# Experts' gathers issued two experts sooner, each in front of the additions of an earlier expert

## The reference, cut to what matters

```python
E, K, D, H, CAP = 32, 4, 512, 256, 256          # T = 8 * 1024 rows
xe = zeros((E, CAP, D)).at[e_flat, pos].set(flat[tok], mode='drop')   # up to 256 rows per expert
h  = relu2(einsum('ecd,ehd->ech', xe, up_w))    # relu, then squared
ye = einsum('ech,edh->ecd', h, down_w)
gathered = ye[e_flat, min(pos, CAP - 1)] * topk_w
routed = gathered.reshape(T, K, D).sum(axis=1)  # each row has 4 experts
out = x + gb * (routed + shared)
```

## Time and profile before

| | us |
|---|---|
| median of 3 runs | 3024.13 (3019.51 to 3024.2) |
| the profiled execution's own time | 2997.19 |
| its span, first to last instruction | 2995.4 |
| PE busy over the span | 2899.0 |
| DVE busy | 2120.9 |
| POOL busy | 1837.7 |
| ACT busy | 1340.9 |

### The profile page before, as it was taken

How to read it: one execution, slowest core, us unless ns; L and a number is a source line. 1 busy time by engine, 2 the same in 40 slices (tenths; PEclk the granted TensorE clock), 3 DMA queues, 4 the chain that set the end, 5 groups by cost and what they waited for, 6 DMA issues and landing times. The chain is left out here.

```text
span 2995.4 us, 49806 instructions
## 1 busy us (share of the span) xinstructions
PE 2899.0 (97%) x16480; PEld 2159.9 (72%) x16480; DVE 2120.9 (71%) x5344; ACT 1340.9 (45%) x2436; POOL 1837.7 (61%) x1077
## 2 busy tenths in 40 slices
PE   8999999999999999999999989999999999989996
PEld 5788888766666666666666578887877888767875
DVE  6555555677777777777777588887878788846764
ACT  2222222156666666666666533223322333236764
POOL 1333222278888888888888157577656776755664
PEclk9999999999999999999999999999999999989998
DMA  7555555755665565555665332333223323148996
GB/s 255 201 193 199 190 182 182 228 122 131 134 136 115 115 134 133 134 116 116 135 136 136 112 127 75 109 100 103 82 80 104 118 84 95 60 142 211 232 237 119
DMA packets 281948, 420.53 MB, mean 140 GB/s; under 512 B 48463, under 2 KB 132687, under 8 KB 281742
## 3 DMA queue, kind: packets, MB, share of 16 engines
q1 hardware_dynamic: 259214, 384.22, 45.2%
q0 software_dynamic: 22528, 33.72, 5.8%
HBM read 263.38 MB, written 153.01 MB: 139 GB/s over the span
## 5 line engine op out<-in xcount | busy, mean ns | idle before, releaser
L1166 ACT ACTIVATE att_pt<-att_ps_p 128x512 f32<-128x512 f32 (+1 forms) x1024 | 524.5, 587 | 192.6 <-PE att_ps_p L1389 168.1
L247 DVE CUSTOM_DVE_ANT_0 att_ps_s<-att_ps_s,att_causal 128x512 f32<-128x512 f32 (+1 forms) x992 | 469.9, 504 | 188.5 <-PE att_ps_s L1304 188.3
L1386 PE MATMUL att_ps_p<-att_qs,att_ks 98*128 98x512 f32 (+3 forms) x1536 | 501.5, 366 | 8.6 <-ACT att_pt L1166 7.8
L1304 PE MATMUL att_ps_s<-att_ks,att_qs 96*128 96x512 f32 x1488 | 505.9, 368 | 2.2 <-DVE att_lower L253 0.6
L1105 POOL TENSOR_TENSOR att_gathered<-att_gathered,att_pt 128x2048 f32<-128x2048 f32 (+1 forms) x92 | 388.3, 4221 | 41.2 <-ACT att_pt L1166 36.4
L253 DVE TENSOR_REDUCE att_lower<-att_ps_s 128x1 f32<-128x512 f32 x496 | 340.0, 685 | 53.0 <-PE att_ps_s L1304 53.0
L1098 POOL TENSOR_TENSOR att_pt<-att_pt 128x1024 f32<-128x1024 f32 (+2 forms) x153 | 331.3, 2165 | 58.6 <-PE att_ps_o L1330 36.8
L1386 PEld LDWEIGHTS att_ps_p<-att_qs,att_ks 98*128 98x128 f32 x1536 | 270.0, 190 | 129.3 <-issue 80.7
L1912 POOL DMA_INDIRECT slot_info<-ffn_info,ffn_slot x256 | 277.2, 1083 | 113.1 <-issue 78.9
L1304 PEld LDWEIGHTS att_ps_s<-att_ks,att_qs 96*128 96x128 f32 x1488 | 273.6, 190 | 69.0 <-DVE att_rowmax L247 22.4
L577 POOL TENSOR_TENSOR qkv_x<-qkv_x,qkv_mod 128x512 f32<-128x512 f32 x60 | 83.5, 1392 | 368.4 <-DVE qkv_x L671 368.4
(11 more groups left out here) (311 smaller groups left out, 6552.2 us busy)
## 6 DMA issues: line engine op xcount, KB each, us to landing
att_qs<-qk_parts SPq DMA_DIRECT2D x96, 512.0 KB, 6.9
att_ks<-qk_parts SPq DMA_DIRECT2D x96, 512.0 KB, 12.8
qk_parts<-qkv_out_hi SPq DMA_DIRECT2D x128, 256.0 KB, 2.2
qk_parts<-qkv_out_lo SPq DMA_DIRECT2D x128, 256.0 KB, 2.4
qkv_x<-x SPq DMA_DIRECT2D x16, 1024.0 KB, 5.5
v_rows<-qkv_out_v SPq DMA_DIRECT2D x64, 256.0 KB, 2.3
att_vs<-v_rows SPq DMA_DIRECT2D x32, 512.0 KB, 16.2
o_parts<-att_o SPq DMA_DIRECT2D x64, 256.0 KB, 7.9
```

The costliest lines, as they stand in the source:

```text
L247: dve.tensor_tensor_reduce(part, part, self.causal[:, UNIT - (c1 - c0):UNIT], scale=1.0, scalar=MASKED, op0=ALU.add, op1=ALU.max, accum_ou ...
L1166: act.activation(tile(c)[:, h, col:UNIT], ps_p[(NPROB * prev.g + n) % NP][:, col:UNIT], ACT.Exp, scale=float(HD) ** -0.5).then_inc(exp_don ...
L1304: pe.matmul(bank("s", cur.g, i)[:, 0:c1 - c0], qs[cur.slot][0:STACK, h, t * P:(t + 1) * P], ks[cur.slot][0:STACK, h, c0:c1], start=True, s ...
L1386: last = pe.matmul(part[:, i * (UNIT - col):(i + 1) * (UNIT - col)], ks[prev.slot][:, h + i, kt * P:(kt + 1) * P], qs[prev.slot][:, h + i, ...
```

## The change

The gathers move by two experts. POOL issues those of experts 4 and 5 ahead of the additions of expert 0, and in step e the gather of e + 6 (into the buffer of e + 2) ahead of the additions of e. DVE copies the row numbers of e + 6 in step e behind the low parts of the turned rows of e + 2, once PE has turned them. As the copies then end six steps before the last, DVE's loop covers 24 steps instead of 28 and the last eight are written out.

```diff
-        def steps(eng, body):
+        def steps(eng, body, tail=1):
             for e in range(-AHEAD, 0):
                 body(e, R + e, -1)
-            with eng.Fori(0, NE // R - 1) as i:
+            with eng.Fori(0, NE // R - tail) as i:
                 for r in ring:
                     body(i * R + r, r, i)
-            for r in ring:
-                body(NE - R + r, r, NE // R - 1)
+            for e in range(NE - tail * R, NE):
+                body(e, e % R, e // R)
...
             def body(e, r):
-                if not isinstance(e, int) or e + R < NE:
-                    relay.gather(pool, e + R, r, h2_dram)
+                if not isinstance(e, int) or e + AHEAD + R < NE:
+                    relay.gather(pool, e + AHEAD + R, (r + AHEAD) % R, h2_dram)
                 add(e, r)
...
+            for e in range(AHEAD):
+                relay.gather(pool, e + R, e, h2_dram)
             body(0, 0)
...
-                if live(e) and live(e + R):
-                    dve.wait_ge(tr_done, CREDIT + 2 * (e + 1))
-                    dve.sem_inc(mark, 1)
-                    dve.tensor_copy(tok_get[r][:, :], tok_all[:, bass.ds((e + R) * J, J)]).then_inc(get_done, 1)
                 if live(e + 2) and live(e):
                     relay.low_up(dve, e + 2, r % 2, (r + 2) % R)
...
+                if live(e + 2) and live(e + 2 + R):
+                    dve.wait_ge(tr_done, CREDIT + 2 * (e + 3))
+                    dve.sem_inc(mark, 1)
+                    dve.tensor_copy(tok_get[(r + 2) % R][:, :], tok_all[:, bass.ds((e + 2 + R) * J, J)]).then_inc(get_done, 1)
                 if live(e + 1):
                     dve.wait_ge(ahi_done, CREDIT + e + 2)
...
-            steps(dve, body)
+            steps(dve, body, tail=2)
```

## The result

The changed kernel took 3072.56 us (median of 4, 3071.11 to 3074.45) against 3024.16 of the kernel before in the same session: a ratio of 1.0146, interval 1.0112 to 1.0179. It is 48 us slower, where 9 were forecast.

What follows compares the result with a forecast made beforehand. The additions' transfers to the output were taken to set the pace. 0.7 + 9.6 - 1.0 = +9.3 us on the profiled 2997.19 gave 3006.5, with 26.9 carried over 3033.4 us; range 3011 to 3043, the forecast's own 3028 to 3044.

Steps and rivals of the forecast that it cites:

- PE's waits for gathers go: PE's transposes: nine waits for gathers, 13.8 us, all vanish, worth nothing by itself since PE doesn't set the pace.
- The gathers on POOL: POOL, between two experts' additions: two issues as before, some 3 us hidden while additions land; cost 0 in the steady part.
- The start: Before expert 0's additions: the gather of expert 6 now stands ahead and delays them; +0.7 us, bounds 0 and +1.3.
- From expert 6 on DVE is locked to A: DVE's result step: waits in every step for landed additions to free a result buffer, tying it to the additions' starts.
- Every load comes about 3.4 us after an A: SP's weight loads: issued about 3.4 us behind the start of an expert's additions, for 20 periods.
- Their length: Those 20 periods between additions' starts: 9.4 us each instead of 8.92, bounds 8.09 and 10.9; +9.6 us.
- The row numbers: DVE's copy of row numbers for the gather, now behind the turned rows' low parts: adds no wait, cost 0.
- The end: Additions of experts 25 and 26, now with no gather beside them: faster, -1.0 us, bounds 0 and -2.1.
- The lock helps: Rival: loads behind the additions' start fill idle time, periods 8.4 or 8.09 us, about 3013 or 3007 us; chance 0.2.
- Nothing moves: Rival: DMA engines have the same bytes to move, periods stay at 8.9 us, 3024 us (3019 to 3029); chance 0.23.
- The lock isn't reached: Rival: another wait keeps PE back, loads stay ahead of additions' starts, periods some 8.6 us, 3018 us; chance 0.07.
- rule of turns: DMA engines alternate between queues packet by packet; spoke against the slowdown term, making periods of 8.4 us likelier than 8.09.

Runs made afterwards that it cites:

- x_before_behind: Kernel before, each weight load from expert 8 on waiting for a POOL count behind the issues of the additions of six experts earlier; ratio 1.0054.
- c_after: The changed kernel, unchanged, run again beside the kernel before on another chip; ratio 1.0134.
- x_gathered: Changed kernel, each weight load from expert 8 on waiting for a POOL count placed between gather and additions; ratio 1.0142 to the kernel before.
- x_landed: Changed kernel, each weight load from expert 8 on waiting until the additions of seven experts earlier have landed; ratio 1.0043 to the kernel before.
- x_alo: Changed kernel, each weight load also waiting until DVE has made the low part of the activations; ratio 1.0004 to the kernel before.
- c_before: The kernel before, unchanged, run again for a second profile; ratio 0.9996.
- x_noload: Changed kernel, weights of experts 4 to 31 not loaded but for two elements per partition; ratio 0.9922 to the kernel before.
- x_split: Changed kernel, loads waiting for the activations' low part and DVE making the down weights' low part behind the turned rows'; ratio 0.9996 to the kernel before.

## Why the prediction was wrong

The direction and the chain of causes were right; the price was not. By the prediction's own steps:

- *PE's waits for gathers go, by itself worth nothing.* Right: 13.8 us of waits became 1.3, and nothing was gained by it.
- *The gathers on POOL, cost 0.* Right: 0.99 and 1.01 us a piece in most steps, while POOL waits for the landing.
- *The start, +0.7.* Slightly wrong: A(0) began 0.89 us behind the end of its y, as before (0.88), so it cost 0. First gather to A(0) was 27.70 us, before 28.49.
- *From expert 6 on DVE is locked to A.* Late by two or three steps: the count of landed additions released y in the way foreseen from A(8). The prediction held A's pace at 8.92 us on the way to the lock; but with the loads still 4.6 to 7.6 us behind A the periods were 8.2 to 9.4 (mean of A(1) to A(7): 60.41 / 7 = 8.63), so PE gained less on them per step. That makes 17 periods and not 20.
- *Every load comes about 3.4 us after an A.* Right: 3.14 to 3.40 from A(9) to A(24), but for A(17) with 2.30, and 3.85 at A(8).
- *Their length: "Nearest are A(16) to A(17), 9.51 us, and A(4)'s 9.41; I take 9.4", bounds 8.09 and 10.9.* **This is the step that failed.** It was 11.03, above the upper bound: 187.47 - 151.02 = +36.5 us in 17 periods, where the term stood at +9.6. What the sum had at nothing is the hold: a low part on DVE beside B adds 0.9 to 1.1 us to POOL's issue, and with the load 3.1 to 3.4 us behind A the weights then go first, which made 12 of the 17 periods 11.74 us long on average. The row that I leaned on was of the other kind. In the kernel before, at A(16):

```profile
2857.86 1.62 POOL L1489 DMA_INDIRECT out<-exp_y,exp_tok_add  x1 [0.30 <-issue]
```

  B took 1.62 us, and the low part began at 2857.95, 0.09 us *behind* it. The row was a free step; 12 of the 17 that it was to stand for were held. I had both rows and didn't put them beside each other. The upper bound came from a step that was itself in part held. In A(7) of the kernel before the low part began 0.68 us ahead of B, B took 1.99 us, and it ended 1.45 us behind the low part. DVE, then POOL:

```profile
2773.79 1.22 DVE L378 TENSOR_TENSOR exp_dn_lo<-exp_dnr,exp_dn_hi 128x1024 fp32r<-128x1024 f32 x1
```

```profile
2774.47 1.99 POOL L1489 DMA_INDIRECT out<-exp_y,exp_tok_add  x1 [0.30 <-issue]
```
- *The row numbers, cost 0.* Possibly wrong in an indirect way. Ahead of the low parts the copy took a little time of DVE: from y to the down weights' low part were 2857.95 - 2855.10 = 2.85 us before, and 2872.76 - 2870.07 = 2.69 at A(13) after. These 0.16 us are what the low part is ahead of B by. That the copy's place decides the race is argued from these rows; a kernel with only the copy moved back wasn't tried. And it isn't needed for a hold: x_before_behind has the copy in its old place, and 11 of its 20 steps were held.
- *The end, -1.0.* Wrong: +1.15. A(25) took 10.60 us, where it took 8.43 before. B was held there too (2.58 us), but no load was issued behind A(24)'s, and from 3008 to 3018 us SP's queue moved nothing, so this isn't the weights going first. A(26), with a B of 2.66, took only 8.66. Why A(25) was slow is open; c_after, x_gathered, x_landed and x_alo have it too (10.0 to 10.9).

Summed: 17 periods +36.45, A(25) to A(31) +1.15, A(0) to A(8) -3.1 give the stage's +34.5 (34.4 between c_after and c_before; the median of c_after is 37 above that of the kernel before on its chip). The measured 48 us have an interval of 34 to 54 (0.0112 to 0.0179 of 3024), so the stage is just within it. What the other 14 us between stage and median were, I can't tell from one profiled execution each; the share ahead of the experts isn't there in the later experiments.

The rivals. *The lock helps*: PE's pace is real (8.17 us in x_noload), but the free steps of c_after with a load at +3.4 took 8.98 us on average (62.83 / 7). *Nothing moves*, with its 8.9, would thus have been right for steps that aren't held. *The lock isn't reached*: it is.

The Trainium skill's rule of turns (DMA: Bandwidth & Descriptors, section "Queues, rings and completion order"), which I weighed as a case in which the lock helps, isn't what a held step shows: one packet of POOL's queue in 3 us beside 672 of SP's. The free step (120 beside 397) could be read as turns. Whether the held descriptors were visible to the engines at that time no run shows.

For the hold, the Trainium skill has a page that I hadn't weighed (SBUF — State Buffer, section "SBUF: two separate sides"): VectorE and GpSimd share a pair of ports, and whichever starts first keeps it for its whole instruction; of VectorE's instructions it names those in a 2-port mode and those with two inputs in SBUF, the latter only against a GpSimd instruction that reads SBUF. The order of starts agrees with most rows above, and so does x_split, where an operation with one input in PSUM didn't hold B. It doesn't fit the low parts that began 0.02 to 0.04 us behind B and held it even so (A(15), A(16) and A(19) after). That POOL's issue reads SBUF at that time no run shows. Had I read the page for the operations beside B, the rival "held" would have stood among mine, with the 10.9 us of A(7) as its nearest price.

What stays open: why a low part that starts 0.02 to 0.04 us behind B holds it in some steps (2.68 or 2.69 us at A(15), A(16) and A(19)) and not in others; why the weights, once first, keep POOL's queue out so fully; and why A(25) was slow with no load beside it.

## What to carry to other kernels

When a wait is removed and two engines become locked to each other, every step repeats one phase, and a race of 0.2 us that the kernel before met in a few steps falls out the same way in most of them. Before pricing a phase by one row of the trace, put the rows of all engines at that moment beside each other and ask by how little they are in that order. If a prefetch then lands in the wrong place, a wait that delays it by a microsecond or two is one line, and here it was worth all of the loss.

## What the runs showed of the hardware

- A subtraction on DVE with both inputs in SBUF (128x1024, 1.22 us) that starts ahead of an indirect transfer's issue on POOL and is still running holds that issue up, to an end 1.43 to 1.46 us behind its own. So the issue, 1.57 us otherwise, took 2.43 to 2.62 us where the subtraction began 0.23 to 0.03 us ahead, 1.99 us at 0.68 (A(7) before), and 1.57 us at 1.10. A subtraction with an input in PSUM, 0.22 us ahead, doesn't hold it.
- The hold is 0.9 to 1.1 us, but cost 3 us and more, as 1 MB of weights issued at that time went through first: POOL's queue moved 1 packet in 3 us. With the weights some 1.9 us later the hold cost nothing that can be measured.
- A count that POOL gives behind an indirect transfer without waiting for it came no later than 0.37 us after the first issue's start (SP's load, which waits for it, was issued then), and each of the two issues takes POOL 1.6 us. It can't be used to time other work by the end of an issue.
- Additions of 256 rows of 2 KB beside no load land 6.8 to 7.4 us behind the start of their first issue in nearly all steps of x_noload.
